# The fp4 feed-forward and its following norm, moved batch by batch into the slots of the first cross-attention

## What is computed

```python
x = x + L0_attn(layernorm(x))            # gated linear attention and a gelu feed-forward
x = x + L0_xattn(layernorm(x), ctx)      # first cross-attention, 16 heads of 64
x = x + L0_ffn(layernorm(x))             # fp4 feed-forward
x = x + L1_attn(layernorm(x))            # self-attention, 16 heads of 16, relative bias
x = x + L1_xattn(layernorm(x), ctx, ctx) # second cross-attention, one head, masked
x = x + L1_ffn(layernorm(x))             # quantised gated feed-forward

# L0_ffn: blocks of 32 columns
amax = max(|xb|);  scale = 2 ** (floor(log2(amax)) - 2) * 2 ** d
q = sign(xb / scale) * fp4_round(clip(|xb / scale|, 0, 6))
y = (scale * q) @ w_q.T + bias
```

## Time and profile before

| | us |
|---|---|
| median of 3 runs | 1540.61 (1540.37 to 1542.14) |
| the profiled execution | 1539.43 |
| its span, first to last instruction | 1537.6 |
| TensorE busy, share of the span | 1295.6 (84%) |
| VectorE busy | 1028.9 (67%) |
| ScalarE busy | 741.0 (48%) |
| GpSimd busy | 226.8 (15%) |
| mean granted TensorE clock | 0.919 |

### The profile page before, as it was taken

How to read it: one execution, slowest core, us unless ns; L and a number is a source line. 1 busy time by engine, 2 the same in 40 slices (tenths; PEclk the granted TensorE clock), 3 DMA queues, 4 the chain that set the end, 5 groups by cost and what they waited for, 6 DMA issues and landing times.

```text
span 1537.6 us, 27248 instructions
## 1 busy us (share of the span) xinstructions
PE 1295.6 (84%) x9826; PEld 1099.3 (71%) x9826; DVE 1028.9 (67%) x2389; ACT 741.0 (48%) x1801; POOL 226.8 (15%) x235
## 2 busy tenths in 40 slices
PE   3989798976999999999999999973479977969419
PEld 3979787876888888888888888752257755759409
DVE  5865575545566666666666666658849986885974
ACT  4442324234555555566655665541146653425563
POOL 3334252524000000000000000000044441000100
PEclk9999898987999999999999999986579998989759
DMA  8100101030000000000000000002100000300001
GB/s 270 47 3 4 38 1 42 0 130 20 10 11 11 11 10 10 10 10 10 10 10 10 10 10 0 1 15 71 50 5 3 2 2 28 107 27 1 0 0 44
DMA packets 34522, 40.45 MB, mean 26 GB/s; under 512 B 4890, under 2 KB 29067, under 8 KB 34443
## 3 DMA queue, kind: packets, MB, share of 16 engines
q1 hardware_dynamic: 33614, 39.24, 8.4%
q10 hardware_dynamic: 828, 0.14, 0.1%
HBM read 35.36 MB, written 4.01 MB: 26 GB/s over the span
## 4 chain that ended last, share of the span: by engine, by line
PE 58%; DVE 14%; issue 4%; ACT 3%; DVEq 0%; POOL 0%; ACTq 0%; POOLq 0%
PE bank L718 10%; PE bank L719 8%; PE bank L720 8%; PE bank L925 5%; PE bank L909 5%; PE bank L917 4%; PE bank L885 4%; DVE amax L2242 2%; PE bank L1110 2%; PE bank L1126 1%; DVE z L1754 1%; PE bank L1140 1%; PE bank L871 1%; PE bank L1076 1%; PE bank L1065 1%
## 5 line engine op out<-in xcount | busy, mean ns | idle before, releaser
L1505 ACT ACTIVATE prob<-bank,nmx 100x361 f32<-100x361 f32 x256 | 142.5, 560 | 124.4 <-DVE nmx L2040 124.4
L2040 DVE TENSOR_REDUCE nmx<-bank 100x1 f32<-100x361 f32 x256 | 124.7, 528 | 44.5 <-PE bank L909 34.0
L1996 DVE TENSOR_TENSOR oTl<-bank,oTh 128x100 fp32r<-128x100 f32 x128 | 33.3, 260 | 120.1 <-ACT oTh L1491 120.1
L661 POOL MEMSET v1z<- 100x1024 f32 x1 | 1.0, 951 | 733.1 <-DVE x L2103 733.1
L718 PE MATMUL bank<-cxTh,wxkh 128*128 128x362 f32 x256 | 99.2, 387 | 0.8 <-DVE kTl L1997 0.7
L925 PE MATMUL bank<-pT,vv 128*64 128x100 f32 (+1 forms) x1536 | 95.5, 260 | 0.7 <-DVE oTl L1996 0.7
L925 PEld LDWEIGHTS bank<-pT,vv 128*64 128x64 f32 (+1 forms) x1536 | 70.3, 138 | 35.9 <-issue 23.2
L2057 DVE TENSOR_SCALAR prob<-prob,rsum 100x361 f32<-100x361 f32 x256 | 92.9, 405 | 4.5
L1491 ACT CAST oTh<-bank 128x100 fp32r<-128x100 f32 x128 | 31.7, 248 | 128.6 <-PE bank L925 128.6
L917 PE MATMUL bank<-ident,prob 100*128 100x100 f32 (+1 forms) x768 | 89.6, 252 | 1.9 <-DVE prob L2057 1.9
L917 PEld LDWEIGHTS bank<-ident,prob 100*128 100x128 f32 (+1 forms) x768 | 84.4, 151 | 7.3 <-DVE prob L2057 2.7
(11 more groups left out here) (378 smaller groups left out, 3776.9 us busy)
## 6 DMA issues: line engine op xcount, KB each, us to landing
cx<-in_ctx_dram SPq DMA_DIRECT2D x32, 128.0 KB, 2.0
xc<-in_ctx_dram SPq DMA_DIRECT2D x32, 128.0 KB
parked_weights<-parking SPq DMA_DIRECT2D x9, 256.0 KB, 5.5
mask_i<-in_mask_BxS_ik_dram SPq DMA_DIRECT2D x16, 141.0 KB
w<-in_L_attn_W_dram SPq DMA_DIRECT2D x2, 1024.0 KB, 13.5
cx<-in_ctx_dram SPq DMA_DIRECT2D x16, 105.0 KB, 2.0
xc<-in_ctx_dram SPq DMA_DIRECT2D x16, 105.0 KB
x<-in_x_dram SPq DMA_DIRECT2D x4, 400.0 KB
```

The lines of the kernel that those rows point to most:

```text
L1505: nc.scalar.activation(prob[:, h % 4, :], bank[S_BANKS[e]][0:T, 0:S], ACT.Exp, bias=nmx[:, h:h + 1], accum_out=psum_[:, h:h + 1]).then_inc ...
L2040: nc.vector.tensor_reduce(nmx[:, h:h + 1], bank[S_BANKS[e]][0:T, 0:S], AX_X, ALU.max, negate=True).then_inc(xa_max, 1)
```

## The change

For each batch j the feed-forward is cut into pieces that stand in slots of the first cross-attention, one to two batches later:

- slot 4 of batch j + 1: `row_moments(j, 0)` (statistics and their aggregate) on VectorE; GpSimd forms the reciprocal deviation by an add and a power of -0.5 (`rstd_of`), in place of ScalarE's root and VectorE's reciprocal
- slot 5: `blocks_scaled`; slot 6: `blocks_clipped`; slot 7: `blocks_quantised`, all VectorE, on one batch of 256 columns
- slot 0 of batch j + 2: `block_transposes` (TensorE), `blocks_copied` (ScalarE); slot 1: `block_product` (TensorE), `block_product_added` (VectorE)
- slot 2: `row_moments(j, 1)` for the next norm, again with `rstd_of`; slot 3: `row_normalised`; slot 4: `row_transposes_2` and `rows_copied` into `zT`

GpSimd adds `bproj` batch by batch (`row_with_bias`). The mirrored products of `relb` stand in slots 0 to 3 of batch 0, and SyncE loads `relb` behind the second context. What can't stand in slots, batches 14 and 15, is interleaved with the start of self-attention. `norm(2)` as a whole is gone, and the old `norm(3)` is now `norm(2)`. SyncE issues the contexts of the second cross-attention when the first is done, and the nine parked pieces only when self-attention is done. The tiles are laid out anew for this. The diff, cut to its core:

```diff
@@ SyncE
-            with sp.Fori(1, B) as b:
-                sp.wait_ge(xa_ct, KD * b)
-                load_ctx(ds(b, 1))
-
-            sp.wait_ge(xa_x, B + 1)
+            sp.wait_ge(xa_ct, KD)
+            load_ctx(1)
             sp.dma_start(mirror[:], a["mirror"]).then_inc(relb_in, 16)
...
+            with sp.Fori(2, B) as b:
+                sp.wait_ge(xa_ct, KD * b)
+                load_ctx(ds(b, 1))
...
+            sp.wait_ge(xa_x, B + 1)
+            for r in range(G):
+                load_1(r, r)
+            sp.wait_ge(a1_x, B)
             sp.wait_ge(park_out, 16 * 9)
...
@@ GpSimd
+            def rstd_of(event, part):
+                nonlocal links
+                links += 1
+                pool.wait_ge(ff_v, event)
+                rstd = frstd[:, part:part + 1]
+                nc.gpsimd.tensor_tensor(rstd, fmoments[:, part, 1:2], eps[0:T, :], ALU.add).then_inc(pool_link, 1)
+                pool.wait_ge(pool_link, links)
+                nc.gpsimd.tensor_tensor(rstd, rstd, minus_half[0:T, :], ALU.pow).then_inc(ff_r, 1)
...
+            rstd_of(1, 0)
+            for j in range(B - 1):
+                rstd_of(2 * j + 2, 1)
+                rstd_of(2 * j + 3, 0)
+                row_with_bias(j)
...
@@ TensorE, pe_pair
+                if p == 1 and not starts:
+                    block_product(b - 2)
...
+                if p == 0 and not starts:
+                    block_transposes(b - 2)
+                if p == 4 and not starts:
+                    pe.wait_ge(xa_x, b + 1)
+                    row_transposes_2(b - 2)
+                if starts and not odd and p < 4:
+                    mirrored(p)
                 if p == 2 and not (starts and not odd):
                     pe.wait_ge(xa_ol, pair - 2)
+                    if not starts:
+                        pe.wait_ge(ff_x, b - 1)
                     output_product(bank[W_BANK])
...
@@ TensorE, self-attention
             def queries_projected(i):
 
-                pe.wait_ge(a1_kb, i + 1)
+                o = bank[Y_BANK if i == 0 else QK_BANK]
+                if i == 1:
+                    pe.wait_ge(ff_x, B)
...
@@ VectorE, dve_pair
+                if p == 2 and not starts:
+                    row_moments(b - 2, 1)
                 if p == 3 and not (starts and not odd):
                     added(b - 1)
+                if p == 3 and not starts:
+                    row_normalised(b - 2)
+                if p == 4 and not (starts and not odd):
+                    row_moments(b - 1, 0)
+                if p == 5 and not (starts and not odd):
+                    blocks_scaled(b - 1)
+                if p == 6 and not (starts and not odd):
+                    blocks_clipped()
+                if p == 7 and not (starts and not odd):
+                    blocks_quantised(b - 1)
                 if odd and not ends:
                     queries_low(PAIRS0 * i + PAIRS0 + p, p, bank[O_BANK])
...
+                if p == 1 and not starts:
+                    block_product_added(b - 2)
...
@@ VectorE, behind the slots
+            block_product_added(B - 2)
+            row_moments(B - 2, 1)
             added(B - 1)
...
+            row_moments(B - 1, 0)
+            row_normalised(B - 2)
+            blocks_scaled(B - 1)
+            blocks_clipped()
+            blocks_quantised(B - 1)
```

More of the change, by code:

```diff
@@ L927, in weighted_pair, with both_transposes, block_transposes, block_product @@
                 mm.then_inc(xa_av, 1)
+            def both_transposes(src):
+                for k in range(KD):
+                    mm = pe.transpose(bank[W_BANK][:, k * T:(k + 1) * T], src[:, k * P:(k + 1) * P], ident[0:T, 0:T])
+                mm.then_inc(ff_t, 1)
+            def block_transposes(j):
+                pe.wait_ge(ff_q, 2 * j + 1)
+                if isinstance(j, int) and j:
+                    pe.wait_ge(ff_c, 2 * j)
+                both_transposes(fq)
+            def block_product(j):
+                pe.wait_ge(ff_c, 2 * j + 1)
+                for k in range(KD):
+                    mm = pe.matmul(bank[W_BANK][0:T, 0:D], fqT[:, k, :], wffn[:, k, :], start=(k == 0), stop=(k == KD - 1))
+                mm.then_inc(ff_mm, 1)
+            def row_transposes_2(j):
+                pe.wait_ge(ff_q, 2 * j + 2)
+                both_transposes(z_row)
+            def mirrored(j):
+                pe.wait_ge(relb_in, 16 * RELB_DMAS)
+                at_least(pe, a1_sb, j)
+                pe.matmul(bank[W_BANK][0:T, 0:4 * T], mirror[:], relb[:, j].rearrange("q h k -> q (h k)"), start=True,
+                          stop=True).then_inc(a1_rb, 1)
             def pe_pair(i, n):
@@ L967, in pe_pair @@
                     k = p - 5
+                    if k == 0 and starts and not odd:
+                        pe.wait_ge(a1_sb, 4)
+                    if k == 0 and not starts:
+                        pe.wait_ge(ff_c, 2 * b - 2)
                     if k == 0:
@@ L1526, in act_pair @@
                     probabilities(pair - 1, (p - 1) % PAIRS0)
+                if p == 0 and not starts:
+                    blocks_copied(b - 2)
+                if p == 4 and not starts:
+                    rows_copied(b - 2, zT[:, :, ds(T * b - 2 * T, T)])
+                if starts and not odd and p < 4:
+                    mirror_copied(p)
             for k, o in enumerate((W_BANK, T_BANKS[0])):
@@ new lines, in blocks_scaled @@
+            def blocks_scaled(j):
+                dve.wait_ge(ff_r, 2 * j + 1)
+                link(nc.vector.tensor_scalar(un[:], row(j), fmoments[:, 0, 0:1], frstd[:, 0:1], ALU.subtract, ALU.mult))
+                link(nc.vector.tensor_reduce(fscale[:], blocks(un[:]), AX_X, ALU.max, apply_absolute_value=True))
+                link(nc.vector.tensor_scalar(fscale[:], fscale[:], 1e-30, None, ALU.max))
+                link(nc.vector.tensor_scalar(finv[:].bitcast(I32), fscale[:].bitcast(I32), EXPONENT, None, ALU.bitwise_and))
+                link(nc.vector.tensor_scalar(fscale[:], finv[:], 0.25, act_scale[0:T, 0:1], ALU.mult, ALU.mult))
+                link(nc.vector.reciprocal(finv[:], fscale[:]))
@@ L2032, in dve_pair, with block_product_added, row_normalised @@
+            def block_product_added(j):
+                dve.wait_ge(ff_mm, j + 1)
+                link(nc.vector.tensor_tensor(row(j), bank[W_BANK][0:T, 0:D], row(j), ALU.add))
+                nc.vector.tensor_tensor(row(j), row(j), bffn[:], ALU.add).then_inc(ff_x, 1)
+            def row_normalised(j):
+                dve.wait_ge(ff_r, 2 * j + 2)
+                nc.vector.tensor_scalar(z_row[:], row(j), fmoments[:, 1, 0:1], frstd[:, 1:2], ALU.subtract, ALU.mult).then_inc(ff_q, 1)
             def dve_pair(i, n):
```

244 lines of the change are left out of this document (126 added, 118 removed).

## The result

The changed kernel takes **1486.46 us** (median of 4 runs, 1482.87 to 1487.46) against 1540.49 in the same runs: ratio 0.9645, 95% interval 0.9625 to 0.9665. It is 54 us faster; forecast were 45.5, the range held it. The profiled execution took 1485.77, its span is 1484.0. In the page of the changed kernel (busy us, share of the span, instructions), VectorE has 11 us more of work than before and TensorE 16 us less, in a span 53.6 shorter. Of its group lines (busy us and mean ns of one, idle us before it and its releaser) two show a wait that is new in its size: TensorE's for `kTl` (10.1 us, before 0.7) and for `qTl` (10.3, before none that shows).

A forecast was written before the change was run, and what follows sets the result against it. TensorE paces the cross-attention slots; a lone VectorE chain bounds feed-forward, norm(2) and self-attention's start. 1539.4 - 93.5 + 22.3 + 21 + 3.1 + 2.5 - 1 = 1493.8; median 1.2 above, so 1495 us, range 1476 to 1520.

The forecast's parts named there:

- serial stretch: From the last head pair's transposes to values_out(0): 115.96 us replaced by 22.5, saving 93.5 us (bounds 89 and 97).
- VectorE in the slots: Added VectorE pieces, 7.4 us per batch in cross-attention slots, charged +22.3 in all: 19.6 in slot 5, 2.7 in the last batch.
- TensorE pieces, batches 2 to 15: block_product and two pairs of transposes in the slots: 1.5 per batch, +21 us (17 to 27).
- mirrored products: The four relb products moved into batch 0 at the full clock: 0.67 + 0.1 each, +3.1 us.
- self-attention: Row 15 work left there: queries_projected(1) waits about 1.2, row_normalised 0.4, copy ahead of keys_projected(2) 0.8; +2.5 us.
- parked weights: Later loads and splits: second cross-attention starts about 6 us earlier, gives 3.5 to 5.5 back; net -1 (-6 to +4).
- Slot 5: Shortest slot: blocks_scaled stalls TensorE 1.4 us per batch, for kTl in even and qTl in odd batches; 19.6 over 14.
- Slots 6 and 7 paying: Rival: small VectorE instructions or links there cost more than assumed, 15 x 2.8 = 42 more, 1537 us; 6%.
- VectorE as the bound: Rival: VectorE bounds every slot, all 7.4 us per batch on the path, 111 in place of 22.3, 1584 us; 4%.
- late reciprocals: Rival: GpSimd's add and power take 6 us, too late for slot 5; 26 more, 1521 us; 5%.
- a row add that blocks: Rival: GpSimd's row add, 0.6 per row, blocks VectorE chains TensorE waits for in the slots; 9 more, 1504 us; 10%.
- Slot 5 is cheap: Rival: hidden gaps behind TensorE's modelled ends take back slot 5's stall, transposes slip into them; 1475 us; 8%.

The follow-up runs named there:

- c1: Against the changed kernel: un and the block maxima (two of blocks_scaled's six instructions) moved from slot 5 to behind kTl of slot 4; 1470.12 us.
- c2: Against the changed kernel: blocks_scaled taken wholly out of slot 5, its moments behind kTl of slot 3, the rest in slot 4; 1461.31 us.
- The held splits: Against the kernel before: GpSimd's splits of the parked weights wait for all 16 rows z of the last norm; 1536.72 us against 1539.74.
- c4: Against the kernel with blocks_scaled out of slot 5: GpSimd's splits of the parked gate and up weights cut into passes over 256 columns; 1458.95 us.

## Why the prediction was right, and where its terms were off

| term | forecast | measured |
|---|---|---|
| serial stretch | -93.5 | -93.9 |
| VectorE in the slots | +22.3 | +23.2 |
| TensorE pieces, batches 2 to 15 | +21 | +15.1 |
| mirrored products | +3.1 | +2.1 |
| clock dip in a slot; slots' start | none | +1.6, +0.5 |
| self-attention | +2.5 | -1.0 |
| parked weights | -1 | -1.3 |
| sum | -45.6 | -53.6 |

**The serial stretch.** 22.09 for 22.5, but by luck: two errors cancel. Nor is it the one VectorE chain of about 25 us that was named as its sign: for 13.7 us TensorE sets the pace, and VectorE is busy for 9.2 of the 22.1. TensorE's part, up to the first add of the output product, took 13.7 where the sum at the low clock with its rebate gives 15.2: the clock was back at about 1073, between the two projections, which are of one size:

```profile
1070.63 2.87 PE L1109 MATMUL bank<-zT,wk 128*128 128x200 f32 x8
...
1073.30 1.64 PE L1123 MATMUL bank<-zT,wq 128*128 128x200 f32 x8
```

VectorE's part took 8.4 for 7.3. The reciprocal deviation was as assumed, 1.0 from the end of the aggregate (1079.36) to `un`; but the plan had put nothing beside it, and GpSimd goes on to the row add and, right behind it, a memset; `un` ends behind both and takes 1.69 in place of 0.40.

```profile
1079.18 0.18 DVE L2119 BATCH_NORM_AGGREGATE fmoments<-fstats 100x2 f32<-100x6 f32 x1
...
1080.29 0.73 POOL L678 TENSOR_TENSOR x<-x,bproj 100x256 f32<-100x256 f32 x1
1080.36 1.69 DVE L2124 TENSOR_SCALAR un<-x,fmoments,frstd 100x256 f32<-100x256 f32 x1 [0.71 <-POOL frstd L673]
1080.96 0.95 POOL L690 MEMSET v1z<- 100x1024 f32 x1
```

**Slot 5.** The step held: 1.47 an even and 1.55 an odd batch for the forecast 1.4, at `kTl` in the one and `qTl` in the other; 21.0 for 19.6 over 14 batches. c1 and c2 show it causally. The last batch cost 2.2 for 2.7. **Slots 6 and 7** cost nothing, and the further passes show that there was cover left for most of 0.46 each. **Slots 1 to 4** cost no VectorE time.

**TensorE pieces**, the largest miss: 1.01 and 1.14 a batch, not 1.5. The product was nearly right (0.8 for 0.95; 0.87 for a second one). The transposes were not: two cost 0.17, and in slot 0 of an even batch nothing, where each pair was put at 0.3. The step that failed read this 0.3 out of the 0.53 of three larger ones in the earlier trace rows. That 0.53 is a busy time with a modelled end, but this explains little: by the starts in the kernel before, from 584.87 to the next group, three still take 0.46.

```profile
585.33 0.41 PE L909 MATMUL bank<-kTh,qTh 64*100 64x362 f32 x2
```

The new ones are smaller (100 columns for 128) and start 0.09 apart in the changed kernel; the next group starts 0.12 behind the first of them. Why they cost even less than their size says, and nothing in the even slot 0, stays open.

```profile
609.61 0.34 PE L959 MATMUL bank<-ident,fq 100*128 100x100 f32 x2
609.73 0.46 PE L745 MATMUL bank<-wxvh,cxTh 128*105 128x512 f32 x1
```

**Self-attention.** The wait was there as forecast: `queries_projected(1)` stands 1.13 for `block_product_added(15)`. What was left out is that the first projections, the scores of batch 0 and the keys of the second pair now run while VectorE still quantises row 15, ahead of mark two, so the stage starts with part of its work done (the first two of these rows); and what TensorE does more there lies beside a VectorE that from 1086 to 1097 waits 0.52 us. The gain is all at the stage's start: from mark two to VectorE's third `v1z` it takes 15.2 (to 1101.40) where before it took 16.3 (to 1153.79). A step that counts what is added to a stage has also to count what left it.

```profile
1078.54 0.94 PE L1150 MATMUL bank<-k1z,q1T 32*100 32x200 f32 x16
...
1080.00 1.54 PE L1109 MATMUL bank<-zT,wk 128*128 128x200 f32 x8
...
1096.16 1.62 PE L1123 MATMUL bank<-zT,wq 128*128 128x200 f32 x8 [1.13 <-DVE x L2149]
```

**Parked weights.** The norm gained 6.4 (forecast 6), what follows gave back 5.1 (3.5 to 7.5). The splits start 9.5 later than before, for 11.5. The held splits and the pieces show why the gain is given back: one long pass on one mask, and a low clock. The masked scores, which the prediction counted among the passes that the splits hold, weren't held where c4 has them beside one.

**The range.** It held, and not because the table's rows cancelled: but for the clock dip, the late start and VectorE's 0.9, every term came out lower than put, TensorE's pieces by 5.9 and self-attention by 3.5.

**Rivals.** Slots 6 and 7 paying, VectorE as the bound, late reciprocals and a row add that blocks: none occurred in the slots, the last two shown by their own runs; in the serial end the row add and the memset behind it did hold `un`, which cost 1.3. "Slot 5 is cheap" fell as put, though its other half, transposes that slip into gaps, was true of the even slot 0. The low clock within the slots, named as outside of every term, came once, for 1.6.

## What to carry to other kernels

Before work goes into a pipeline's slots, read for every slot the idle time of the engine ahead of each of its instructions: here 1.75 us cost 1.5 a batch in the one slot without room and nothing one and two slots earlier, and that was worth 25 us, 1.6 of them a clock dip, on top of the 54 of the whole move. Price pipelined matmuls by the distance of their starts. When a pass of another engine may be hit by long ones of GpSimd, cut the long ones up: the mask's 3.46 became 0.75 at most.

## What the runs showed of the hardware that was not expected

- Ten tiny VectorE instructions ahead of a hardware loop made each of its five jumps back cost some 2.3 us of VectorE, 7.9 us of TensorE's slots in all. So an edit anywhere ahead of a loop or in it can look slow for its place alone, as the further passes in slots 6 and 7 did; the sign is an idle time with "issue" as its releaser at the top of the loop.
- A stall of 1.4 to 1.5 us in an otherwise full TensorE now and then brought the granted clock down (0.79 over 8 us) and cost 1.6 more: once in the changed kernel, three times with the product doubled, four times with ten short instructions ahead of the loop, once with further passes in slots 6 and 7, never with short ones in the loop, and in no kernel whose stalls were 0.5 us. Taking a stall away can give more than its own length.
- A 0.35 us VectorE pass took 3.46 beside a GpSimd pass of 3.45, and 0.75 when it met a sixth of it. A VectorE pass with two inputs wasn't held (0.56 for 0.54).
- GpSimd's power of one column took 0.55 us and its add 0.19; with the way there and back 1.0.
